# Layer norm statistics taken per group of four tiles, in an eight-core attention and mixture-of-experts layer on Trainium2

## The reference

```python
def _layernorm(x, axis=-1, eps=1e-5):
    m = jnp.mean(x, axis=axis, keepdims=True)
    v = jnp.var(x, axis=axis, keepdims=True)
    return (x - m) / jnp.sqrt(v + eps)

def _L0_attn_ref(x, Wq, Wk, Wv):            # x (8, 2048, 1024), W (1024, 1024)
    q = jnp.einsum('bnd,de->bne', x, Wq)
    k = jnp.einsum('bnd,de->bne', x, Wk)
    v = jnp.einsum('bnd,de->bne', x, Wv)
    scores = jnp.einsum('bqe,bke->bqk', q, k)
    scores = jnp.where(causal, scores, -jnp.inf)
    attn = jax.nn.softmax(scores / jnp.sqrt(1024.0), axis=-1)
    return jnp.einsum('bqk,bke->bqe', attn, v)

x = x + _L0_attn_ref(_layernorm(x), Wq, Wk, Wv)
x = x + _L0_ffn_ref(_layernorm(x), ...)     # shared expert + 8 experts, top 2, width 2048
```

## Time and profile before

| what | us |
|---|---|
| median of 2 runs | 3792.09 |
| the two runs | 3560.12 and 4024.06 |
| the profiled execution | 3555.22 |
| its span, slowest core (core 0) | 3553.7 |
| its spans, all cores | 3543.7 to 3553.7 |

### The profile page before, as it was taken

The page is one execution under the profiler, slowest core; times in us unless marked ns, Lnnn a source line. Parts: engine busy times, 40 slices in busy tenths (PEclk is TensorE's granted clock), DMA queues, the critical chain, the costliest instruction groups (busy, mean ns, idle before and its releaser), DMA issues.

```text
span 3553.7 us, 40929 instructions; the slowest of 8 cores (3543.7 to 3553.7 us)
## 1 busy us (share of the span) xinstructions
PE 3348.3 (94%) x15960; PEld 1546.6 (44%) x15960; DVE 751.9 (21%) x1195; ACT 562.6 (16%) x1068; POOL 286.0 (8%) x336
## 2 busy tenths in 40 slices
PE   2797769999999999999999999999999999999999
PEld 1354334444444444444444444444444444444444
DVE  3003432121122222222121212122212122221222
ACT  4334431010101010111101010101010111101010
POOL 0000001010101010001001010101010101001000
PEclk9799989999999999999999999999999999999999
DMA  6012008362925382555337342826291546347452
GB/s 143 3 23 24 1 1 107 36 71 25 122 33 72 41 114 25 71 66 77 48 48 101 42 61 35 119 29 79 36 118 25 71 57 86 43 53 94 85 71 60
DMA packets 327625, 214.54 MB, mean 60 GB/s; under 512 B 6928, under 2 KB 301840, under 8 KB 327440
## 3 DMA queue, kind: packets, MB, share of 16 engines
q0 software_dynamic: 323024, 195.14, 43.0%
q1 hardware_dynamic: 4416, 16.78, 1.4%
HBM read 398.63 MB, written 8.39 MB: 115 GB/s over the span
## 4 chain that ended last, share of the span: by engine, by line
PE 91%; DMA 3%; DVE 3%; issue 2%; ACT 2%; DVEq 0%; ACTq 0%; POOL 0%; SPq 0%; POOLq 0%
PE psE L693 14%; PE psF L693 14%; PE psA L640 14%; PE psC L650 14%; PE psD L650 14%; PE psB L640 14%; DMA R<-x 1%; DMA WBUF<-uw 1%; PE psC L478 1%; PE psD L478 1%; DVE R L494 1%; PE psA L280 1%; ACT XQ L250 1%; DVE lst L197 1%; PE psA L336 0%
## 5 line engine op out<-in xcount | busy, mean ns | idle before, releaser
L640 PE MATMUL psA<-XQ,WBUF 128*128 128x512 bf16 x2304 | 547.2, 380 | 11.2 <-DVE KBUF L672 7.2
L650 PE MATMUL psC<-XQ,WBUF 128*128 128x512 bf16 x2304 | 545.2, 379 | 0.0
L640 PE MATMUL psB<-XQ,WBUF 128*128 128x512 bf16 x2304 | 544.3, 379 | 0.0
L650 PE MATMUL psD<-XQ,WBUF 128*128 128x512 bf16 x2304 | 544.3, 379 | 0.0
L693 PE MATMUL psE<-VBUF,KBUF 128*128 128x512 bf16 x2304 | 520.7, 379 | 20.3 <-DVE KBUF L672 20.3
L693 PE MATMUL psF<-VBUF,KBUF 128*128 128x512 bf16 x2304 | 520.8, 379 | 0.0
L663 ACT ACTIVATE gscr<-psA 128x512 bf16<-128x512 f32 x288 | 172.0, 597 | 1795.0 <-PE psA L640 1556.3
L672 DVE TENSOR_TENSOR KBUF<-gscr,psC 128x512 bf16<-128x512 bf16 x288 | 198.0, 687 | 805.1 <-PE psC L650 737.7
L672 DVE TENSOR_TENSOR KBUF<-gscr,psD 128x512 bf16<-128x512 bf16 x288 | 198.0, 687 | 792.7 <-PE psD L650 774.0
L693 PEld LDWEIGHTS psE<-VBUF,KBUF 128*128 128x128 bf16 x2304 | 224.1, 98 | 296.3 <-issue 28.6
L640 PEld LDWEIGHTS psA<-XQ,WBUF 128*128 128x128 bf16 x2304 | 225.0, 98 | 287.3 <-issue 20.8
(11 more groups left out here) (134 smaller groups left out, 1068.3 us busy)
## 6 DMA issues: line engine op xcount, KB each, us to landing
WBUF<-gw POOLq DMA_DIRECT2D x128, 512.0 KB, 7.3
WBUF<-uw POOLq DMA_DIRECT2D x128, 512.0 KB, 9.1
VBUF<-dw POOLq DMA_DIRECT2D x32, 1024.0 KB, 16.4
R<-x SPq DMA_DIRECT2D x4, 2048.0 KB, 23.9
WBUF<-sgwT POOLq DMA_DIRECT2D x16, 512.0 KB, 9.1
WBUF<-suwT POOLq DMA_DIRECT2D x16, 512.0 KB, 11.2
out<-R SPq DMA_DIRECT2D x16, 512.0 KB, 2.6
VBUF<-sdwT POOLq DMA_DIRECT2D x4, 1024.0 KB, 17.8
```

The lines of the kernel that those rows point to most:

```text
L640: ts=ts, gb=gb, tbase=tbase: e.matmul(gb[:, :], wgrp[:, pp, 0, hc, ic * 128:(ic + 1) * 128], XQ[:, hc, tbase + ts * 512: tbase + (ts + 1) ...
L650: ts=ts, ub=ub, tbase=tbase: e.matmul(ub[:, :], wgrp[:, pp, 1, hc, ic * 128:(ic + 1) * 128], XQ[:, hc, tbase + ts * 512: tbase + (ts + 1) ...
```

## The change

The loop that takes the statistics of all 16 tiles is removed, and each group of the K stage takes the statistics of its own four tiles first. Every instruction is the same as before; only their order on ScalarE and VectorE changes, and nothing on TensorE, GpSimd or SyncE.

```diff
-    for tt in range(NTT):
-        ln_stats(tt, v_pre=0, v_dx=t_xc[tt // 4])
     qkv_banks = (psA, psB, psC, psD)
     bi = 0
     wait("tensor", dWw, t_wk)
     xq_ready_s = 0
     for ts in range(4):
+        for tt4 in range(4):
+            tt = 4 * ts + tt4
+            ln_stats(tt, v_pre=0, v_dx=t_xc[tt // 4])
         for tt4 in range(4):
             tt = 4 * ts + tt4
             ln_fin_a(tt)
```

## The result

| what | before | after |
|---|---|---|
| ratio of the two, with its 95% interval | | 1.0037 (1.0023 to 1.0051) |
| median over all runs | 3662.7 (42 runs) | 3573.66 (43 runs) |
| lowest run | 3553.7 | 3570.05 |
| profiled execution | 3555.22 | 3574.12 |
| spans of its cores | 3543.7 to 3553.7 | 3562.1 to 3572.6 |

The changed kernel is slower by 0.37%, that is by 13 us of 3557 (8 to 18 by the interval); the two lowest runs differ by 16.4 us. Between a third and over half of the runs of each kernel have the cores of a die at a lower clock and take up to 4238 us, and the ratio leaves those out, so the two medians are not to be compared.

What follows compares the result with a forecast made beforehand. Bound by memory waits before the first K matmul, then by the serial ScalarE, VectorE, TensorE chain between K groups, with TensorE busy in nearly all slices; -1.9 + 15.45 + 0.3 = +13.9 us, forecast 3571, range 3546 to 3592.

Steps and rivals of the forecast that it cites:

- The level: Whole kernel: 13.9 us added to recorded runs of 3555.22 and 3560.12, giving 3571 us, 0.4% up, likeliest "no difference".
- The sum: Whole kernel: -1.9 at the start, +15.45 for squares in three gaps, +0.3 for slower transposes, together +13.9 us.
- What goes away: Start, before the first K matmul: early Ln gains only 1.9 us, because the first transpose waits for wk; bounds 0 and 30.4.
- What is added: Gaps between K groups: four squares ahead of Ln on ScalarE cost 5.15 us each, 15.45 us for three; transposes 0.3 more.
- The rival that squares cost nothing: Gaps between K groups: unseen slack absorbs the squares, total change -1.9 us, 3555 us; chance 5%.
- the one on table loads: Gaps between K groups: squares between copies and Ln force table loads, at most +7.7 us in all, 3579 us; chance 2%.
- The ramp: First chain of each K group: slow clock start not made worse by longer idle; 0 us, bounds -0.5 and +1 per group.
- The rival on the clock: K groups: clock stays down, other seven chains take 3.5 us, +37 in three groups, +51 total, 3608 us; chance 4%.
- The V stage and after: From the V stage on: same instructions and waits, everything only shifted by 13.9 us.
- the wait for wk doesn't bind: Start: wk is early or its wait releases early, full 30.4 us gained, total change -14.7, 3542 us; chance 7%.
- the bound of 0 for the squares: One gap between K groups: 0 us if squares slipped into ScalarE's idle time between evictions; held excluded by its in-order queue.

Runs made afterwards that it cites:

- the second experiment: Changed kernel with TensorE's wait for wk moved from ahead of the first transpose to ahead of the first K matmul; ratio 1.0006 to the kernel before.
- the first experiment: Changed kernel with the next group's squares and sums written between evictions of the group before, not after all eight; ratio 0.999 to the kernel before.
- the sixth: Version with squares between evictions and moved wk wait, x's chunks 1 to 3 now issued only after wk landed; ratio 0.9942 to the kernel before.

## Why the prediction's sum was right, and its level wrong

**The step that failed** is the one headed "The level". The sum gave +13.9 us, that is a slower kernel. The prediction then added it to the lower one of the recorded runs (3555.22 and 3560.12 were its anchors) and said 3571, beside a recorded median of 3792.09. Against that median 3571 is a kernel that is 5.8% faster, the opposite of the sum. The same step went on "this is 0.4% up; a measurement of this kernel tells about 2% from no change, so the likeliest answer is 'no difference'". The runs showed a slowdown in place of both: 0.37%, with an interval of 0.23 to 0.51% that leaves "no change" outside, and lowest runs of 3553.7 before and 3570.05 after. The interval is 0.14% wide to either side, so 0.4% can be told. The forecast should have been a ratio, 1.004 with bounds around it, and its sign should have been stated as the result. That 3571 lies near the median after, 3573.66, is luck in part: the same median of the kernel before is 3662.7, with a lowest run of 3553.7.

The mechanism held, term by term.

- *What goes away.* The prediction said that wk and not the early Ln would set the first transpose. The row after says "51.65 <-DMA WBUF<-wk", and moving the wait took 12 us away beyond what an earlier landing gave, while the same edit in the kernel before took nothing. The term was -1.9 and came out at -0.8 (the mean over the cores), as wk landed 0.8 us later in that execution (46.7 us from its issue in the mean, against 45.9). With that added back, it is -1.6. The rest is a misread delay: the prediction took 0.1 us from a landing to the instruction that waits for it, read on VectorE and x, and TensorE started 0.35 us after wk's landing (51.30 and 51.65 on core 3, 0.35 in the mean too).
- *What is added.* 5.15 us per gap was read from three rows; ScalarE's Ln moved by 5.15 in the gap shown. The second and third gap grew by 5.2, of which some 0.1 is the slower first transposes, and the first by 5.6, of which 0.4 is not explained (see the end): 16.0 in all where the sum had 15.75. Doubling the squares added the same again, and hiding them took all of it away. The rival that squares cost nothing is out. So is the one on table loads: the changed kernel has one at line 207, as before, and none between the groups.
- *The ramp* was taken as 0 with bounds of -0.5 and +1 per group. The four groups took 1.0 us more in sum. The difference is mostly in the second chain, psB, which takes 1.73 to 3.04 us from start to start over the groups of the six cores whose records are complete (2.39 in the mean), where it took 1.73 to 2.97 (2.04) before. The prediction read 1.81 on core 0 and let that core speak for all; core 6 of the kernel before already had this (67.13 and 70.49 are starts, and the third chain starts at 73.47):

```profile
67.13 3.57 PE L280 MATMUL psA<-XQ,WBUF 128*128 128x512 bf16 x8 [0.80 <-ACT XQ L250]
70.49 3.14 PE L280 MATMUL psB<-XQ,WBUF 128*128 128x512 bf16 x8
73.47 1.89 PE L280 MATMUL psC<-XQ,WBUF 128*128 128x512 bf16 x8
```

  So a slow second chain was there before, on some cores. That the longer gaps caused the 1.0 us is not shown: with gaps another 5.5 us longer the groups took 2.1 us less. The rival on the clock, with seven slow chains in a group, is out: the third chain of a group takes 1.73 us on every core.
- *The V stage and after* were to be only shifted. The 1.7 us more that came there in this pair of executions are within what executions differ by.

In sum the V stage begins 16.3 us later where the prediction had 13.9: 1.1 of the 2.4 us between them are the first term, 1.0 the ramp and 0.3 the gaps. The ratio's 13 us lie closer to 13.9 than that, and part of this closeness is chance, since its interval reaches from 8 to 18.

Two smaller steps fell with the runs. The rival "the wait for wk doesn't bind" had a gain of 30.4 us for the case that wk is early. It would have been some 21 at most: the constants' semaphore, raised last by rwT at 28.5 to 33 us in the second experiment, would have held the first transpose. The wait stands in ln_fin_b (line 235), and the trace has the landing; only the wait that ended last was read, not the one below it. And the bound of 0 for the squares ("its queue, which is in order, excludes that") is true for the order that was written, but the same squares written elsewhere cost nothing, as the first experiment shows.

## What to carry to other kernels

An instruction that is moved earlier gains only what lies between its old place and the next wait on its way; list all the waits of the first consumer, with their landing times, and not only the one that ended last. What is moved out of a stretch that waits for memory loses its cover, and on an in-order queue it then costs its full time at each place where it lands on the serial chain: here 12 squares, free beside the loads, cost 16 us between the groups, and nothing again when written between the evictions. Where the effect is small and single runs spread, forecast a ratio with its sign, and do not set an absolute number from one level beside a median from another.

## What the runs showed of the hardware that was not expected

- A load of 16 KB on GpSimd's queue (rwT) landed 29.6 us after its issue while x was being loaded, and after 10.8 us when only a quarter of x was; wk, 2048 KB in SBUF, took 45.8 and 22.8 us there (core 7 of the second experiment, core 1 of the sixth).
- The granted clock fell to 0.50 at the start of a K chain, behind a gap in which it had been at 1.00 throughout with TensorE busy for 9.68 of 14.5 us. Three gaps filled in the same way gave one fast group and two with a slow start on every core, and not at the same place on all.
- With the squares doubled and the gaps at 25.5 to 26.2 us, the K groups were 2.1 us shorter in sum than with gaps of 20.0 to 20.5.
- In the first K group the profile shows a granted clock of 1.00, and yet the first chain took 3.57 us, the same as at 0.50 later. The stretch of that chain in the changed kernel (columns as in the earlier trace rows) is below. The next chain starts 3.57 us after it, at 67.48, so the duration is real and the record of the clock does not fit it.

```profile
63.91:67.48 3.57, 3.57 (x9) 1.28 (x10) 3.19 (x6) 0.00 (x0) 0.00 (x0) 1.00 0.00 0
```

- In the changed kernel the first gap was 0.3 to 0.4 us longer than the other two on all six cores whose records are complete, and in the kernel before on none of its six; in the timeline the xlntm of its third tile starts 0.4 us late behind its Exp. That wasn't explained.
